# First attention of a decoder: softmax denominators turned into columns and inverted there, spread back by TensorE; maxima turned in one transpose

## The reference

```
x = x + tanh(g_xattn[0]) * attention(layernorm(x), ctx, ctx)
```

## Time and profile before

| | us |
|---|---|
| median of 3 runs (lowest, highest) | 3678.72 (3677.7, 3682.36) |
| profiled execution, first to last instruction | 3689.2 |
| first score matmul to last addition of the first attention, profiled | 160.3 to 588.4 |
| VectorE's turn items of tiles 2 to 29, first start to last start, profiled | 211.2 to 546.6 |

### The profile page before, as it was taken

One profiled execution on the slowest core, in us unless ns is written; L12 is line 12 of the kernel. 1 busy time (PEld: TensorE's weight loads), 2 busy tenths in 40 slices (PEclk: granted clock), 3 DMA queues, 4 the chain that ended last, 5 costly groups with the idle time before them and its releaser, 6 DMA issues. The chain is left out here.

```text
span 3689.2 us, 60303 instructions
## 1 busy us (share of the span) xinstructions
PE 2870.5 (78%) x20178; PEld 1835.6 (50%) x20178; DVE 2185.6 (59%) x4954; ACT 1479.2 (40%) x3032; POOL 1095.9 (30%) x1490
## 2 busy tenths in 40 slices
PE   5388884476699995559957698999989649999993
PEld 4223332332355553423323486454568538888782
DVE  7689993577577776634468687888868620000003
ACT  5267772154222224659945454222245211111110
POOL 2111110177233335512269543000034441111110
PEclk7599996599899997569978899999989659999996
DMA  8766644299522223378600252000044221111204
GB/s 261 177 116 119 122 107 140 69 367 361 175 80 80 79 81 133 128 126 128 114 1 1 91 170 65 1 1 1 1 140 143 87 62 56 48 55 50 85 28 137
DMA packets 261609, 386.10 MB, mean 105 GB/s; under 512 B 56865, under 2 KB 188942, under 8 KB 261056
## 3 DMA queue, kind: packets, MB, share of 16 engines
q1 hardware_dynamic: 234480, 312.50, 31.7%
q0 software_dynamic: 25152, 68.22, 5.3%
q10 hardware_dynamic: 1680, 1.57, 0.2%
HBM read 227.49 MB, written 160.24 MB: 105 GB/s over the span
## 5 line engine op out<-in xcount | busy, mean ns | idle before, releaser
L3125 POOL DMA_INDIRECT rows_out<-e_out,e_tr_dest x224 | 234.9, 1048 | 875.9 <-DVE e_out L3755 514.1
L1195 ACT ACTIVATE a_pt<-a_psS 128x512 f32<-128x512 f32 x512 | 277.5, 595 | 155.5 <-PE a_psS L1093 151.1
L3755 DVE COPY e_out<-e_psD 128x512 f32<-128x512 f32 x40 | 27.7, 692 | 496.3 <-PE e_psD L3723 496.1
L1217 DVE TENSOR_REDUCE a_mx_sb<-a_psM 128x4 f32<-128x1024 f32 x256 | 293.1, 1215 | 18.9 <-PE a_psM L1076 17.7
L3523 PE MATMUL e_psG<-e_wgu,e_yT 128*128 x576 | 275.1, 600 | 25.8 <-ACT e_yT L3551 23.2
L1107 PE MATMUL a_psV<-a_pt,a_vt 128*18 128x256 f32 x4096 | 292.2, 387 | 2.0 <-issue 1.6
L3723 PE MATMUL e_psD<-e_w,e_hT 128*128 128x256 f32 x1280 | 293.3, 389 | 0.0
L3712 PE MATMUL e_psH<-e_yT,e_w 128*128 128x256 f32 x1280 | 285.4, 381 | 1.6 <-issue 0.8
L3655 ACT ACTIVATE e_hT<-e_psH 128x512 f32<-128x512 f32 x160 | 95.5, 597 | 456.4 <-PE e_psH L3712 453.1
L3723 PEld LDWEIGHTS e_psD<-e_w,e_hT 128*128 128x128 f32 x1280 | 248.2, 196 | 34.2
L3712 PEld LDWEIGHTS e_psH<-e_yT,e_w 128*128 128x128 f32 x1280 | 244.8, 191 | 35.8 <-issue 2.1
(11 more groups left out here) (428 smaller groups left out, 6110.2 us busy)
## 6 DMA issues: line engine op xcount, KB each, us to landing
kbd<-e_bgu SPq DMA_DIRECT2D x64, 512.0 KB
cr_kbd<-kbd SPq DMA_DIRECT2D x64, 512.0 KB, 3.4
rows_in<-zeros POOLq DMA_DIRECT2D x36, 522.0 KB, 6.6
e_xin<-rows_in SPq DMA_DIRECT2D x144, 128.0 KB
vbd<-e_bd SPq DMA_DIRECT2D x64, 272.0 KB
cr_vbd<-vbd SPq DMA_DIRECT2D x64, 272.0 KB, 2.7
cq_rows<-rows_out SPq DMA_DIRECT2D x32, 512.0 KB, 5.9
e_w<-in_L_ffn_w_dram SPq DMA_DIRECT2D x16, 1024.0 KB, 7.6
```

Of the source, the lines that this page charges most:

```text
L1195: act.activation(pt[:, probs(t, h), b, :, :], psS[:, unit(t, h, b) % S_BANKS, :].rearrange("p (k c) -> p k c", k=KC), ACT.Exp, scale=scale ...
L1217: dve.tensor_reduce(mx[:, t % 2, :, h, :], psM[:, k % 2, :, :].rearrange("p b (f c) -> p b f c", f=2), AX_X, ALU.max).then_inc(ring_read, 1)
L3125: pool.indirect_dma_start(out=self.rows_out[0:limit, :], out_offset=bass.IndirectOffsetOnAxis(ap=self.dest[:, t:t + 1], axis=0), in_=rows, ...
```

## The change

The numerators are gathered as before, but the denominators take another way, spread over two turn items (`SCALE_LAG` = `LEAD` + 1, so the result of tile t is made in the turn item of tile t+3 instead of t+2):

- In the turn item of tile t, TensorE turns the maxima with one transpose of 32 columns instead of two of 16. It then computes the denominators of tile t-2 with `turn_sums`: four float32 matmuls whose stationary operand is a 128x128 block of `ov` and whose moving operand has 8 columns, so that they land as 128x32. The gather has two matmuls instead of four. Last, `spread_inverses` takes the inverted denominators of tile t-3, repeated 8 times, as 128x64 stationary operands against the identity (four float32 matmuls of 128 moving columns).
- VectorE's shifts work on 32x128 instead of 16x256, its reciprocal on 128x32 instead of 128x256. The multiplication takes the numerators from SBUF and the spread inverses from PSUM.
- ScalarE copies the numerators from PSUM to SBUF (`copy_numer`), after the exponentials of head 2. TensorE waits for that copy before it fills the slot again.
- GpSimd repeats the inverses (`widen`, 128x32 to 128x256) after its addition; the addition of a tile waits one turn item longer.
- SyncE issues eight DMAs for the shift rows instead of four, each of half the columns.
- There is one turn item more after the last tile.

```diff
+    SCALE_LAG = LEAD + 1
...
-        mx = core.sb(ctx, n + "_mx_sb", [P, 2, 2, HEADS, 2], F32)
-        sh = core.sb(ctx, n + "_sh_sb", [PAIR, 2, 2, DIM], BF16)
+        mx = core.sb(ctx, n + "_mx_sb", [P, 2, 2, 2, HEADS], F32)
+        sh = core.sb(ctx, n + "_sh_sb", [2 * PAIR, 2, 2, P], BF16)
         ov = core.sb(ctx, n + "_ov_sb", [P, 2, 2, DIM], F32)
-        rec = core.sb(ctx, n + "_rec", [P, 2, DIM], F32)
+        rec = core.sb(ctx, n + "_rec", [P, 2, 2, KC, HEADS] if with_max else [P, 2, DIM], F32)
+        numer = core.sb(ctx, n + "_numer", [P, 2, DIM], F32) if with_max else None
+        wide = core.sb(ctx, n + "_wide", [P, 2, 2, KC, HEADS, HD], F32) if with_max else None
...
+        def copies_before(k):
+
+            return sum(1 for t in range(LEAD, TILES + LEAD) if turn_item(t) <= k)
...
-                        pool.wait_ge(ring_read, turn_item(t + LEAD) + 1)
+                        pool.wait_ge(ring_read, turn_item(t + SCALE_LAG) + 1)
...
+                def widen(t):
+                    pool.wait_ge(inverted, t + 1)
+                    if t >= 2:
+                        pool.wait_ge(turned, t - 2 + SCALE_LAG + 2)
+                    pool.tensor_copy(wide[:, t % 2, :, :, :, :].rearrange("p b k h d -> p (b k h) d"),
+                                     rec[:, t % 2, :, :, :].rearrange("p b k (h d) -> p (b k h) d", d=1).broadcast_to([P, 2 * KC * HEADS, HD])).then_inc(widened, 1)
...
+                    if with_max and t >= SCALE_LAG:
+                        widen(t - SCALE_LAG)
...
+                    if with_max and t + 1 < TILES:
+                        widen(t + 1)
...
-                            sp.dma_start(at_tile(qa, slice(row, row + 1), t, slice(0, HEADS)),
-                                         sh[HEADS * b:HEADS * (b + 1), t % 2, s, :]).then_inc(shift_loaded[t % 2], 16)
+                            for f in range(2):
+                                rank = PAIR * f + HEADS * b
+                                sp.dma_start(at_tile(qa, slice(row, row + 1), t, slice(0, HEADS), slice(f * P, (f + 1) * P)),
+                                             sh[rank:rank + HEADS, t % 2, s, :]).then_inc(shift_loaded[t % 2], 16)
...
+                    if copies_before(k - 2):
+                        pe.wait_ge(numer_copied, copies_before(k - 2))
...
-                    for f in range(2):
-                        ins = pe.transpose(bank[0:PAIR, f * P:(f + 1) * P], mx[:, t % 2, :, :, f].rearrange("p b h -> p (b h)"), core.ident[:, :])
-                    return ins
-
-                def gather(t, out):
+                    return pe.transpose(bank[0:2 * PAIR, 0:P], mx[:, t % 2, :, :, :].rearrange("p f b h -> p (f b h)"), core.ident[:, :])
+
+                def gather(t, out, parts):
                     pe.wait_ge(out_done, t + 1)
-                    for d in range(2):
+                    for d in range(parts):
                         for b in range(2):
                             ins = pe.matmul(out[HALF * b:HALF * b + HALF, d * DIM:(d + 1) * DIM], pick[:, d, :, :, :].rearrange("p g q d -> p (g q d)"),
                                             ov[:, t % 2, b, :], start=True, stop=True, tile_position=(0, HALF * b))
                     return ins
 
+                def turn_sums(t, out):
+
+                    pe.wait_ge(out_done, t + 1)
+                    for b in range(2):
+                        for k in range(KC):
+                            u = (b * KC + k) * HEADS
+                            ins = pe.matmul(out[:, u:u + HEADS], ov[:, t % 2, b, k * P:(k + 1) * P],
+                                            pick[:, 1, :, :, 0].rearrange("p g q -> p (g q)"), start=True, stop=True)
+                    return ins
+
+                def spread_inverses(t, out):
+
+                    pe.wait_ge(widened, t + 1)
+                    for b in range(2):
+                        for k in range(KC):
+                            ins = pe.matmul(out[HALF * b:HALF * b + HALF, k * P:(k + 1) * P],
+                                            wide[:, t % 2, b, k, :, :].rearrange("p h d -> p (h d)"),
+                                            core.ident[:, :], start=True, stop=True, tile_position=(0, HALF * b))
+                    return ins
+
                 def turn_and_gather(t):
 
                     k = turn_item(t)
                     pe.wait_ge(ring_read, k - 1)
+                    if copies_before(k - 2):
+                        pe.wait_ge(numer_copied, copies_before(k - 2))
                     if t + 1 < TILES:
                         ins = turn_max(t + 1, psM[:, k % 2, 0, :])
-                    if 0 <= t - LEAD:
-                        ins = gather(t - LEAD, psM[:, k % 2, 1, :])
+                    if 0 <= t - LEAD < TILES:
+                        turn_sums(t - LEAD, psM[:, k % 2, 0, P:])
+                        ins = gather(t - LEAD, psM[:, k % 2, 1, :], 1)
+                    if 0 <= t - SCALE_LAG:
+                        ins = spread_inverses(t - SCALE_LAG, psM[:, k % 2, 0, DIM:])
                     ins.then_inc(turned, 1)
...
-                    turn_and_gather(TILES)
-                    turn_and_gather(TILES + 1)
+                    for t in range(TILES, TILES + SCALE_LAG):
+                        turn_and_gather(t)
...
+                def copy_numer(t):
+                    act.wait_ge(turned, t + LEAD + 2)
+                    if t >= 2:
+                        act.wait_ge(ring_read, turn_item(t - 2 + SCALE_LAG) + 1)
+                    act.activation(numer[:, t % 2, :], psM[:, turn_item(t + LEAD) % 2, 1, 0:DIM], ACT.Copy).then_inc(numer_copied, 1)
...
+                        if with_max and t >= LEAD and h == 2:
+                            copy_numer(t - LEAD)
...
-                    dve.tensor_reduce(mx[:, t % 2, :, h, :], psM[:, k % 2, :, :].rearrange("p b (f c) -> p b f c", f=2), AX_X, ALU.max).then_inc(ring_read, 1)
+                    dve.tensor_reduce(mx[:, t % 2, :, :, h], psM[:, k % 2, :, :].rearrange("p b (f c) -> p f b c", f=2), AX_X, ALU.max).then_inc(ring_read, 1)
 
                 def shifts(t, bank):
                     if t >= 2:
-                        dve.wait_ge(shift_loaded[t % 2], 64 * (t // 2))
-                    dve.tensor_scalar(sh[:, t % 2, 0, :], bank[0:PAIR, 0:DIM], -1.0, None, ALU.mult).then_inc(hi_done, 1)
+                        dve.wait_ge(shift_loaded[t % 2], 128 * (t // 2))
+                    dve.tensor_scalar(sh[:, t % 2, 0, :], bank[0:2 * PAIR, 0:P], -1.0, None, ALU.mult).then_inc(hi_done, 1)
                     dve.wait_ge(hi_done, t + 1)
-                    dve.scalar_tensor_tensor(out=sh[:, t % 2, 1, :], in0=bank[0:PAIR, 0:DIM], scalar=-1.0,
+                    dve.scalar_tensor_tensor(out=sh[:, t % 2, 1, :], in0=bank[0:2 * PAIR, 0:P], scalar=-1.0,
                                              in1=sh[:, t % 2, 0, :], op0=ALU.mult, op1=ALU.subtract).then_inc(shift_ready, 1)
...
+                def shift_and_scale(t):
+                    bank = psM[:, turn_item(t) % 2, :, :]
                     dve.wait_ge(turned, t + 2)
                     if t + 1 < TILES:
-                        shifts(t + 1, psM[:, k % 2, 0, :])
-                    if 0 <= t - LEAD:
-                        divide(t - LEAD, psM[:, k % 2, 1, 0:DIM], psM[:, k % 2, 1, DIM:2 * DIM], ring_read)
+                        shifts(t + 1, bank[:, 0, :])
+                    if 0 <= t - LEAD < TILES:
+                        if t - LEAD >= 2:
+                            dve.wait_ge(widened, t - LEAD - 1)
+                        dve.reciprocal(rec[:, (t - LEAD) % 2, :, :, :],
+                                       bank[:, 0, P:P + 2 * KC * HEADS].rearrange("p (b k h) -> p b k h", b=2, k=KC)).then_inc(inverted, 1)
+                    u = t - SCALE_LAG
+                    if u >= 0:
+                        if u >= 2:
+                            dve.wait_ge(added, u - 1)
+                        dve.wait_ge(numer_copied, u + 1)
+                        dve.tensor_tensor(res[:, u % 2, :], numer[:, u % 2, :], bank[:, 0, DIM:2 * DIM], ALU.mult).then_inc(ring_read, 1)
                     else:
                         dve.wait_ge(shift_ready, t + 2)
+                        if t - LEAD >= 0:
+                            dve.wait_ge(inverted, t - LEAD + 1)
                         dve.sem_inc(ring_read, 1)
...
```

More of the change, by code:

```diff
@@ L914, in phase_attend @@
     shift_loaded = [core.sem(f"{n}_sl{m}") for m in range(2)]
-    turned, ring_read, shift_ready, hi_done = (
-        core.sem(n + k) for k in ("_tu", "_rr", "_sr", "_hi"))
+    turned, ring_read, shift_ready, hi_done, widened, numer_copied = (
+        core.sem(n + k) for k in ("_tu", "_rr", "_sr", "_hi", "_wi", "_nc"))
     exp_done, pv_done, out_done, gathered, v_laid, made, cleared, gated, inverted, scaled, added, ones_set = (
@@ L1083, in scores_t @@
                         if with_max:
-                            pe.wait_ge(shift_loaded[t % 2], 64 * (t // 2 + 1))
```

(36 more changed lines are left out.)

## The result

The change is slower: 3714.47 us (3713.75 to 3717.1, four runs) against 3680.54 us (3677.7 to 3683.85, four runs of the kernel before beside it), a ratio of 1.0089 [1.0072, 1.0106]. That is +33.9 us where +5.4 was predicted, and it lies above the predicted range.

The account below looks back on a forecast made before the run. A loop of VectorE's turn item, seven reductions and PE's item was taken to set the 12.4 us period. 27 x (-0.21 + 0.10) = -3 and ends of +8.4 gave +5.4 on 3678.7: 3684 us, range 3667 to 3704.

Parts of the forecast that it names:

- VectorE's item: VectorE's work in each turn item: 2.90 to 1.26 us, with the reciprocal at 0.37.
- `scores_t` of head 4 behind `copy_numer`: TensorE's scores after ScalarE's copy: a stall of 0.26 us; nothing if the copy hides, 0.4 if it waits.
- the way from item to item: From the end of PE's turn item to the start of its next: 9.93 us.
- Gather and spread: Matmul passes at the end of PE's turn item: 1.15 us for both together (0.9 to 1.5).
- at the full granted clock: Engine busy times in the first attention were read at the full granted clock, 2.4 GHz.
- The shift rows: DMAs before `scores_t` of head 0: landing 7.75 us after PE's item, costing 0.1 a period (0 to 1.2).
- mechanism C: Rival: shift rows land late at `scores_t` of head 0, periods 0.6 us longer, 3698 us (3706 if later); chance 0.30.
- The ends: Start, tiles 30 and 31, and tail of the first attention: +2.5, +2.5 and +3.4, together +8.4 us (4 to 11).
- The tail from the last sums: From the last sums to the last addition of the first attention: +3.4 us.
- it competes with the last shift DMAs: GpSimd's DMA of zeros, issued some 3.3 us after PE's item instead of 8.8, competes with the last shift DMAs.
- Rival D: Slower: loads of PE's spread don't hide, 0.5 us more a period, PE's item over 2.7, 3699 us; chance 0.05.
- Rival B: Faster: PE's item shorter than priced, the copy hides, shift rows in time; 3662 us, likeliest 3669; chance 0.20.

Follow-up runs that it names:

- experiment 4: The changed kernel with four shift-row DMAs and `turn_sums` issued twice: 3755.05 us with 8 moving columns, 3745.82 us with 32.
- experiment 3: The kernel before with only one transposition and shifts of 32x128: 3677.37 and 3675.72 us with four shift-row DMAs, 3690.46 us with eight.
- experiment 1: The changed kernel with four shift-row DMAs instead of eight, run twice: 3685.35 us (ratio 0.9977) and 3680.91 us (0.998).

## Why the prediction was wrong

**Item by item it was close.** VectorE's item 1.31 (1.26 said), reciprocal 0.34 (0.37), `scores_t` of head 4 behind `copy_numer` 412.84 - 412.49 = 0.35 after the scores before it, where 411.62 - 411.39 = 0.23 is usual, so held up by 0.12 (0.26 said), the way from item to item 9.89 (9.93). The sums took 0.89 from start to start (0.96). Gather and spread together took 410.51 - 409.44 = 1.07 (1.15). The period was therefore 11.97 at full clock, 0.23 under the forecast.

**The step that failed: "at the full granted clock".** The sum priced PE's item at 2.4 GHz, as the rows of before showed it, and had no term for a clock that the change itself lowers. That term is 23.8 us of the miss. Two causes are shown: more passes of the sums without any late row (experiment 4), and waits of over 1 us without the new denominators (experiment 3). What the change has is mostly the two together. The sums and the spread with rows in time lose only 5.5 and 2.5 us to the clock (experiment 1). In the change run again, the same reckoning gives 6.0 for waits and 16.8 for the clock. In its first profile four of the five chains of low periods begin with a late row. Neither forecast nor rivals held this term.

**The shift rows: mechanism C was at work, with a smaller wait than it said and a cost behind the wait that it didn't have.** The last issue was to start 5.45 after PE's item; the eight took 5.73 in all (5.38 said), 0.72 each, so it started 0.72 + 5.73 - 0.72 = 5.73 after. In calm periods the rows landed at 7.58 (said 7.75), which cost nothing; the slack was 0.26 and not 0.4, so the limit lay at 7.60 and not at 7.76. The forecast made it one value per period; in fact it scatters, from no wait to 1.71, and comes to 6.0 us over the 27 periods, 0.22 each, where the sum took 2.7 and C 16. C priced each late period at its wait; what it missed was the clock behind the wait.

**The ends.** Start +4.1 (said +2.5): the eight small DMAs and the queue behind them, as described, only longer. For the rest +10.4 instead of +5.9. The tail from the last sums took 8.63 instead of 6.27 before, +2.4 (said +3.4). But the burst of five zeros now goes out beside the shift rows of tile 30, and the wait is 5.2 longer. The step that failed there is "it competes with the last shift DMAs", named for the steady stretch and not followed to the tiles where five go out at once. The burst alone doesn't do it: with four issues instead of eight the same burst went out as early (540.49 to 544.24, 2.7 behind VectorE's item) and PE had no such wait, and with eight issues and the zeros put back the wait was 3.9.

The miss adds up: clock 23.8, waits 6.0 - 2.7 = 3.3, start 1.6, end 4.5, less 27 x 0.23 = 6.2 for the shorter period: 27.0; measured 32.1 - 5.4 = 26.7. The 0.3 between them is one period of before that took 12.71. That the price of the period came out 0.23 too high hid 6.2 us of the miss, which is luck.

**Rival D** is refuted. The Trainium skill's rule ("TensorE: Matmul & The Clock Gate", "The mechanism"), that a load overlaps only where its row group differs, does not hold here: the spread's eight passes, loads filling all rows, took 410.51 - 409.92 = 0.59, and their loads are recorded from 409.70 to 410.33, beside running passes. D needed an item of over 2.7; it is 2.08. **Rival B**, a faster kernel, needed a period under 11.86; with the shift rows in time and the clock at full the periods come to 11.97, not quite there, and experiment 1 is a little faster than before.

**What the denominators' new way is worth.** With four DMAs, the whole change has a phase of 416.8 to 422.7 in four runs, the maxima part alone 414.1 and 414.3. The 1.32 us that the new denominators save VectorE (2.63 to 1.31) buy 0.07 a period (11.97 against 12.04), 2 us in all; the end is 3 longer, and the low periods take the rest. TensorE takes over as the bound: it is busy 11.26 of 11.97 us. The maxima part alone with four DMAs is faster than both kernels, by 0.45% and 0.31% against the one before and by over 1% against the change, each measured against the kernel before.

## What to carry to other kernels

When work is moved from VectorE to TensorE in a loop where TensorE is already 86% busy, look not only at the added length but at the granted clock after it. Here eight more passes that mostly load stationary operands cost 0.9 by themselves and 1.8 more through the clock (experiment 4), and in the change the clock took 23.8 us where the waits for late rows took 6.0. Merge small DMAs on the way to the critical matmul before anything else; splitting four into eight cost 17 to 38 us, and a partition step merged them back for nothing. Test the parts of a change one by one: here the modest part, with four DMAs, was worth all of the gain.

## What the runs showed of the hardware

- The granted clock can fall with no idle time just ahead: in the windows at 475 and 416 us PE is recorded busy throughout and the clock is at 0.50, 2.0 and 1.5 us after PE's last idle time of 0.47 and 0.37. It rises again about 3 us later.
- Small SBUF to SBUF DMAs on SP took 0.72 each to issue in the changed kernel, and 0.53 to 0.62 each as four with a step of 64 partitions; with those no steady wait for shift rows was left.
- Not settled: what in the sums lowers the clock. A wider moving operand alone doesn't prevent it. Whether fewer or smaller stationary loads would avoid it was not tried, nor were the spread's passes tried without the sums, and the fall differs from run to run of the same code (six and three periods in experiment 1, 20 and 14 in the change).
